# The expert map one unit earlier, with added constant products, in a fused attention and expert layer

## What is computed

```python
xn = _layernorm(x, axis=-1)
# attention: 16 heads of 16, windows of 128 at a stride of 64, rows cut back to 512
qkv = (xn @ w_qkv + b_qkv)
probs = jax.nn.softmax(scores, axis=-1)
o = o @ w_out + b_out
# experts
topk_scores, topk_idx = jax.lax.top_k(scores, TOP_K)      # 2 of 8
hidden = jax.nn.silu(h1) * h2
y = jnp.sum(total_probs[..., None] * expert_out, axis=-2)
x = x + attention(xn) + experts(xn)
```

## Time and profile before

| | |
|---|---|
| median of 3 runs (lowest to highest) | 743.64 us (742.49 to 745.95) |
| the profiled execution | 746.3 us, span 744.5 us |
| its mean granted TensorE clock | 0.976 |
| PE busy | 666.6 us of 744.5 |
| DVE busy | 565.8 us of 744.5 |

### The profile page before, as it was taken

One profiled execution on the slowest core, in us unless ns is written; L12 is line 12 of the kernel. 1 busy time (PEld: TensorE's weight loads), 2 busy tenths in 40 slices (PEclk: granted clock), 3 DMA queues, 4 the chain that ended last, 5 costly groups with the idle time before them and its releaser, 6 DMA issues.

```text
span 744.5 us, 17166 instructions
## 1 busy us (share of the span) xinstructions
PE 666.6 (90%) x5648; PEld 517.6 (70%) x5649; DVE 565.8 (76%) x881; ACT 512.1 (69%) x886; POOL 307.7 (41%) x334
## 2 busy tenths in 40 slices
PE   0686786969999999999999999999988998989995
PEld 0564564847878787778777887888766676767674
DVE  4758899657777777777777787778758879797984
ACT  4665486556767676767676767666756787978885
POOL 3000373422544454445444544454411244656654
PEclk9999798869999999999999999999999999999999
DMA  9894688370111111111111111111136777976740
GB/s 289 262 241 163 155 287 279 87 254 28 54 45 49 49 51 47 49 49 49 49 50 49 49 49 49 49 49 48 51 103 188 219 228 197 265 212 188 202 158 29
DMA packets 66351, 92.56 MB, mean 124 GB/s; under 512 B 6432, under 2 KB 53408, under 8 KB 66304
## 3 DMA queue, kind: packets, MB, share of 16 engines
q1 hardware_dynamic: 57872, 70.40, 31.7%
q0 software_dynamic: 6864, 18.75, 7.9%
q10 hardware_dynamic: 1568, 2.76, 1.2%
HBM read 59.06 MB, written 32.83 MB: 123 GB/s over the span
## 4 chain that ended last, share of the span: by engine, by line
PE 64%; DVE 11%; ACT 9%; issue 8%; DMA 3%; POOL 3%; SPq 1%; ACTq 0%; DVEq 0%; POOLq 0%
PE PS L1266 57%; PE PS L1516 4%; DVE SMALL L960 3%; ACT WORK L803 3%; PE PS L1494 2%; DVE XN L1122 1%; ACT QS L798 1%; DVE WALL L954 1%; DMA XN<-in_x 1%; POOL OTS L603 1%; DVE WORK L1032 1%; DVE WORK L1025 1%; DMA KS<-parts_scratch 1%; DVE WALL L978 1%; ACT WORK L731 1%
## 5 line engine op out<-in xcount | busy, mean ns | idle before, releaser
L370 DVE TENSOR_TENSOR WS<-WALL,WS 128x1024 fp32r<-128x1024 f32 x144 | 176.4, 1225 | 91.1 <-ACT WS L886 90.5
L1266 PE MATMUL PS<-WS,XTS 128*128 128x512 f32 x852 | 236.4, 413 | 2.4 <-DVE XTS L954 2.3
L1266 PEld LDWEIGHTS PS<-WS,XTS 128*128 128x128 f32 x852 | 151.6, 191 | 46.8 <-DVE XTS L954 14.9
L886 ACT ACTIVATE WS<-WALL 128x1024 fp32r x144 | 152.2, 1058 | 41.5 <-issue 39.3
L1266 PE MATMUL PS<-WALL,WORK 128*128 x568 | 136.2, 383 | 0.8 <-ACT WORK L902 0.8
L666 POOL DMA_INDIRECT WORK<-xn_scratch,WORK x72 | 101.2, 1406 | 31.6 <-issue 21.4
L1266 PEld LDWEIGHTS PS<-WALL,WORK 128*128 128x128 f32 x568 | 102.2, 190 | 12.9 <-issue 1.0
L603 POOL TENSOR_TENSOR OTS<-SIDE,XN 128x256 f32<-128x256 f32 x31 | 26.2, 845 | 195.7 <-DVE XN L1122 116.1
L670 POOL DMA_INDIRECT ys_scratch<-SIDE,WORK x36 | 42.0, 1165 | 118.6 <-ACT SIDE L912 118.6
L960 DVE TENSOR_REDUCE SMALL<-PS 128x8 f32<-128x1024 f32 x64 | 77.4, 1209 | 13.5 <-PE PS L1266 12.9
L803 ACT ACTIVATE WORK<-PS 128x512 f32<-128x512 f32 x128 | 69.4, 595 | 20.3 <-PE PS L1266 16.6
(11 more groups left out here) (142 smaller groups left out, 1008.6 us busy)
## 6 DMA issues: line engine op xcount, KB each, us to landing
WALL<-in_wexp SPq DMA_DIRECT2D x28, 384.0 KB, 7.0
WALL<-ys_scratch SPq DMA_DIRECT2D x16, 512.0 KB, 7.0
parts_scratch<-WORK SPq DMA_DIRECT2D x32, 240.0 KB, 2.4
QS<-parts_scratch SPq DMA_DIRECT2D x16, 480.0 KB, 4.5
XN<-in_x SPq DMA_DIRECT2D x4, 1024.0 KB, 12.3
xn_scratch<-XN SPq DMA_DIRECT2D x4, 1024.0 KB, 7.5
WALL<-in_x SPq DMA_DIRECT2D x8, 512.0 KB, 5.6
KS<-parts_scratch SPq DMA_DIRECT2D x16, 240.0 KB, 3.8
```

The source lines that it names most:

```text
L370: eng.tensor_tensor(out=WS[:, 1 - k, half, 1], in0=weights, in1=WS[:, 1 - k, half, 0].bitcast(F32), op=ALU.subtract).then_inc(low_ready[ha ...
L886: act.activation(WS[:, 1 - k, half, 0], weights, ACT.Copy).then_inc(high_ready[half], 1)
L1266: return pe.matmul(o, a, b, start=start, stop=stop)
```

## The change

The map's products are written behind unit 3 of batch 1 on PE, behind its projection; they were behind unit 4, ahead of unit 5. DVE takes and finishes the map in unit 4 (`take_map` was there already, `finish_map` was in unit 5). `keep_warm` is a new function of PE alone: products of the constants `IDF` and `WOUT` whose result nobody reads. Two of them stand ahead of every even unit from batch 0's unit 4 to batch 1's unit 6 (six places), behind a wait for `r_free`; two more stand at the entry of the expert phase and three on either side of the last projection, which now follows the first two `tokens` and has its reciprocal and division in halves. `rows_out` is one semaphore for each batch: ACT waits for the first before `high_part(1, 1, 0)`, DVE for the second before `low_part(1, 1, 0)`. ACT's `high_part(0, 0, 1)` moves behind the two `take_xt`.

```diff
-MAP_UNIT = 4
+MAP_UNIT = 3
+WARM_FROM = 4
...
         @block.scalar
...
                 high_part(0, 0, 0)
-                high_part(0, 0, 1)
                 act.wait_ge(probs_ready, c["ST"].now() + 2)
...
                 take_xt(0, 0)
                 take_xt(1, 1)
-                act.wait_ge(rows_out, 16 * EXTRA)
+                high_part(0, 0, 1)
+                act.wait_ge(rows_out[0], 16)
                 high_part(1, 1, 0)
...
         @block.vector
...
-                        if u == MAP_UNIT:
+                        if u == MAP_UNIT + 1:
                             take_map()
-                        if u == MAP_UNIT + 1:
                             finish_map()
...
-                    if last and u == UNITS - 1:
-                        invert_last()
+                    if ends(b) and u == UNITS - 1:
+                        invert_halves()
...
-                if ends(b):
-                    if not last:
-                        invert()
+                if last:
                     project(b, NWIN - 1)
...
                 low_part(dve, 0, 0, 0)
-                dve.wait_ge(r_free, c["R"].now() + 1)
...
                 low_xt(0, 0)
                 low_xt(1, 1)
+                project(EXTRA - 1, NWIN - 1)
+                dve.wait_ge(r_free, c["R"].now() + 1)
                 low_part(dve, 0, 0, 1)
+                dve.wait_ge(rows_out[1], 16)
                 low_part(dve, 1, 1, 0)
                 hidden(0, 0)
...
         @block.tensor
...
+            def keep_warm(o, n):
+
+                for _ in range(n):
+                    mm(o, IDF[:], WOUT[:, 0, :])
...
                 for u in range(UNITS):
+                    if first is not None and u % 2 == 0 and b * UNITS + u >= WARM_FROM:
+                        pe.wait_ge(r_free, c["R"].now() + 1)
+                        keep_warm(R_BANK[:, 0:D], 2)
...
-                    if first == 1 and u == MAP_UNIT:
-                        slot_map()
-                    if first == 1 and u == MAP_UNIT + 1:
+                    if first == 1 and u == MAP_UNIT + 2:
                         pe.wait_ge(map_taken, 1)
                     if u % 2 == 1 and (u > 1 or (b and b != EXTRA)):
                         project()
-                if ends:
+                    if first == 1 and u == MAP_UNIT:
+                        slot_map()
+                if last:
                     project()
...
-                pe.wait_ge(r_full, c["R"].now())
+                pe.wait_ge(w_free, c["W"].now() + 1)
+                keep_warm(W_BANK[:, 0:D], 2)
...
                 tokens(0, 0)
                 tokens(1, 1)
+                keep_warm(W_BANK[:, 0:D], 3)
+                project()
+                keep_warm(W_BANK[:, 0:D], 3)
                 up(0, 0, 0)
                 up(0, 0, 1)
```

More of the change, by code:

```diff
@@ L329, in layer @@
         xt_full, xt_high, xt_free = sem("xt_full"), sem("xt_high"), sem("xt_free")
-        rows_out = sem("rows_out")
+        rows_out = [sem(f"rows_out{b}") for b in range(EXTRA)]
         high_ready = [sem("high_ready0"), sem("high_ready1")]
@@ L483, in keep @@
                 t = slice(b * TB, (b + 1) * TB)
-                sp.dma_start(rv[:, t, :], XN[:, t, :]).then_inc(rows_out, 16)
+                sp.dma_start(rv[:, t, :], XN[:, t, :]).then_inc(rows_out[b], 16)
             begin(0)
@@ L496, in _ @@
             keep(1)
-            sp.wait_ge(rows_out, 16 * EXTRA)
+            for b in range(EXTRA):
+                sp.wait_ge(rows_out[b], 16)
             sp.wait_ge(y_stored, 1)
@@ L600, in divide @@
                 pool.wait_ge(sides_ready, 2 * w + 2)
-                pool.wait_ge(recip_ready, w + 1)
+                pool.wait_ge(recip_ready, w + 1 + (w >= EXTRA * NWIN))
                 wait_some(pool, r_full, w)
@@ L604, in divide, with divide_halves @@
                                    ).then_inc(turned_ready, 1)
+            def divide_halves(w):
+                pool.wait_ge(sides_ready, 2 * w + 2)
+                pool.wait_ge(r_full, w)
+                for k in range(NC_D):
+                    pool.wait_ge(recip_ready, w + 1 + (w >= EXTRA * NWIN) + k)
+                    pool.tensor_tensor(out=OTS[:, k, :], in0=SIDE[:, k * P:(k + 1) * P],
+                                       in1=DENS[:, k * P:(k + 1) * P], op=ALU.mult).then_inc(turned_ready, 1)
             def combine(t, first, ready):
@@ L678, in _ @@
             divide(6)
-            divide(7)
+            divide_halves(7)
             pool.wait_ge(xt_full, 1)
@@ L698, in _ @@
                         divide(b * NWIN + n)
[L699 to L704, removed]
+            divide_halves(B * NWIN - 1)
         @block.scalar
@@ L808, in sides @@
                 act.wait_ge(o_full, n)
-                wait_some(act, turned_ready, n - 1)
+                wait_some(act, turned_ready, n - 1 + (n > EXTRA * NWIN))
                 act.activation(SIDE[:], O_SUMS, ACT.Copy).then_inc(sides_ready, 1)
@@ L1122, in invert, with invert_halves @@
                 dve.reciprocal(out=DENS, in_=DENS).then_inc(recip_ready, 1)
-            def invert_last():
+            def invert_halves():
                 n = c["O"].add()
@@ L1400, in project @@
             def project():
-                pe.wait_ge(turned_ready, c["R"].now() + 1)
-                pe.wait_ge(r_free, c["R"].now() + 1)
+                n = c["R"].now()
+                before = n + (n >= EXTRA * NWIN)
+                pe.wait_ge(turned_ready, before + 1)
+                pe.wait_ge(r_free, n + 1)
                 for ch in range(NC_D):
-                    if c["R"].now() == B * NWIN - 1 and ch:
-                        pe.wait_ge(turned_ready, B * NWIN + ch)
+                    if n in (EXTRA * NWIN - 1, B * NWIN - 1) and ch:
+                        pe.wait_ge(turned_ready, before + 2)
                     last = mm(R_BANK[:, 0:D], OTS[:, ch, :], WOUT[:, ch, :], ch == 0, ch == NC_D - 1)
@@ L1436, in batch @@
             def batch(b, first=None):
-                par, last, ends = b % 2, b == LAST, b in (EXTRA - 1, LAST)
+                par, last = b % 2, b == LAST
                 for u in range(UNITS):
+                    if first is not None and u % 2 == 0 and b * UNITS + u >= WARM_FROM:
+                        pe.wait_ge(r_free, c["R"].now() + 1)
+                        keep_warm(R_BANK[:, 0:D], 2)
                     if not last:
```

## The result

The changed kernel takes 767.34 us (766.68 to 768.43, 4 runs), the kernel before in the same comparison 744.80 us (742.49 to 746.86, 4 runs): a ratio of 1.0301 with a 95% interval of 1.0276 to 1.0325, 22.5 us slower. The prediction was 764.8 us, 752 to 770, which is 21.2 us more than the 743.64 us that it started from. The profiled execution has a span of 766.0 us, 21.5 more than before.

A forecast was written before the change was run, and what follows sets the result against it. DVE was taken as the limit from 92 to 126 us, kept full by PE's lead. Even units 15.8, map 3.0 and entry 2.4 sum to 21.2 us, bringing the median of 743.64 to about 764.8 us, range 752 to 770.

The forecast's parts named there:

- What bounds the stage: From 92 to 126 us DVE is the limit, busy 32.81 of 34.00 us, and PE waits for it.
- The lead is lost by the wait: At even units PE can't begin before DVE ends the unit before, so DVE idles for PE's next products.
- The even units: DVE stalls at batch 0's units 4 and 6, batch 1's units 0 and 2: 15.8 us, between 10.6 and 17.1.
- The map: Behind unit 3 of batch 1: starts 1.4 us earlier, but unit 4's scores, maximum and reciprocal queue behind it; net 3.0 us lost.
- The entry: Start of the expert phase: the last projection follows the token tiles and the rows' store is waited for; 2.4 us lost.
- the cover: Batch 1's units 4 to 7 end within 13.16 us of the map's end, hiding unit 6's wait; otherwise it costs 2 us.
- the rows' store: At the entry, SP's store of the rows needs the 5.66 us that it needed before.
- The signs: Changed profile: DVE idle 2 to 5 us at even units, map directly behind POOL's places, loads at about 165.5 us.
- One sign of being wrong: First token tile not coming 13 us behind the last experts' loads but waiting for the attention work.
- The rival with the upper clock: Products keep PE's clock up through the batches; stalls 10.6, map 3.0, entry about 1: 14.6 us, 758 us; chance 0.22.
- The faster rival: PE's clock was the price; DVE doesn't wait in even units, and 7.7 us are gained: 736 us; chance 0.05.

The follow-up runs named there:

- a1: Changed kernel without the r_free waits and the two constant products at the six even units; new map place and entry stay: 750.82 us, ratio 1.0058.
- c4: As a1, but with the wait and its two products at batch 1's unit 2 alone: 756.36 us, ratio 1.0143.
- b2: As a1, but with the map behind unit 4's scores: 744.33 us, ratio 0.9993.
- c1: Changed kernel, all as it is, but with the map behind unit 4's scores: 763.56 us, ratio 1.0219.
- c3: As a1, with six constant products added between unit 3's projection and the map: 749.85 us, ratio 1.0053.
- a4: Changed kernel with the map back behind unit 4 and its lists finished in unit 5; waits, products and new entry stay: 767.92 us, ratio 1.0288.
- b1: Kernel before with the changed kernel's entry alone; map in its old place, nothing at the even units: 748.50 us, ratio 1.0040.
- b4: As b2, but without the eight constant products of the entry: 743.47 us, ratio 0.9984.
- c2: Kernel before with only the r_free waits and two products ahead of the six even units; map and entry as before: 767.54 us, ratio 1.0293.
- b3: Kernel before with only the map moved behind unit 4's scores and its lists finished in unit 4: 745.14 us, ratio 0.9998.

## Why the prediction was right, step by step

**What bounds the stage: shown.** DVE was the limit from 92 us to the map, and it had no slack: with the waits and products gone (a1) 18.1 us come back, with one wait and its pair (c4) 5 us go.

**The lead is lost by the wait and not by the products: shown.** Measured on a1, the waits alone cost 11.4 us, the products alone 3.3, both together 18.1. What PE makes for the next unit and what DVE does last in this one overlapped before; the wait makes them follow each other.

**The even units, 15.8 us: measured 15.7.** The terms were 5.6, 2.1, 3.6 and 4.5, and came out as 4.3, 2.0, 5.0 and 4.5. For unit 4 of batch 0 I had added 0.9 for ScalarE's chain, which had slack, and the clock rose before the scores. In batch 1's unit 0 I took the middle between full and half clock, and it was half; I also forgot ScalarE's part, 0.53 us with its wait, between the queries and keys and DVE's split. The errors cancel, which is luck. One slip besides: for unit 4 of batch 0, 92.81 and 2.1 + 1.7 + 1.0 make 97.6 and not 97.5, and 4.9 us and not 4.7.

**The map, 3.0 us: measured 5.2 (21.24 less 16.0).** The start of the map (1.4 us early in the sum, 1.6 measured against the shift of 16.0) and what is queued behind it (4.4 net in the sum, 4.3 measured) were right; a1, b2 and c1 show that the second is unit 4's scores, maximum and reciprocal. The term that is missing is the map's clock:

```profile
152.00:159.00 7.00, 6.61 (x65) 0.59 0.47 125
...
181.00:186.00 5.00, 4.47 (x23) 1.00 0.25 68
```

In the first stretch, the map's, the granted clock is 0.59, in the second, the entry's, 1.00. PE had waited for POOL's places for 3.26 us, the map started at the lower of its two levels (1.2 GHz), and 4.2 us became 6.7. In the kernel before, PE went into the map straight from unit 4 at 1.00. c3 shows that it is this gap: filled, the map takes 4.2 us. The other runs agree: 4.2 us where PE goes into the map from work at full clock (a4, b1, b4, c2), 5.5 to 6.7 behind waits of 2.2 to 3.6 us. By the Trainium skill (TensorE: Matmul & The Clock Gate, "HAM oscillation — how this bites in real kernels") waits between bursts of products bring the lower clock back; the trace agrees here and ahead of three of the four pairs of constant products. I had used that rule for the products and not for the map that I had moved behind a wait.

**The entry, 2.4 us: measured 0.2.** The token tiles came 0.6 us late of the loads (13.79 us in place of 13.16, because the attention work with unit 6's stall, 3.4 us, now ended last: the cover was gone by that much), and the first hidden tile 0.4 us earlier behind them. Two things make the difference. The mis-sized term is the rows' store: I took 5.66 us from issue to release, which in the kernel before lay beside the end of the experts' loads (DMA share 0.91 and 0.80 in the 4 us from 158), and in the changed kernel, with 0.43 and 0.74 from 184, DVE went on 3.77 us after the issue. In the twelve other kernels it was 3.62 to 3.89. (The 3.4 us in b1's expectation are counted from the end of the issue.) That the loads beside it made the difference was not tried by itself, but b3 and c2 speak for it: they have the entry of the kernel before, issue the store 16.2 and 13.8 us behind the loads in place of 12.7, and both show 3.62. The other thing is the clock. b1 shows that the entry does cost 2.0 us where PE has waited for the weights; in the changed kernel the late attention work kept PE busy, and the clock was 1.00. I had not foreseen that the entry is cheap where the attention work ends last.

**The signs.** DVE was idle 2.6 to 5.0 us in the four even units, the map stood behind POOL's places, and DVE waited 1.8 us for the rows' store, as foreseen. The loads came at 167.74 and not at 165.5. One sign of being wrong did appear: the token tiles waited for the attention work, 0.6 us beyond the 13.16. The sum had priced batch 1's unit 6 at nothing as long as the cover held, and it didn't hold.

So the mechanism was right for the even units, which are three quarters of the cost, and two smaller terms were wrong by 2.2 us each, in opposite directions. That the sum of 21.2 us came out so close to the 21.5 of the spans (22.4 by the ratio) is in that part luck. **The rival with the upper clock** (758 us) failed at its first step: two constant products for each even unit don't keep the clock up when the wait in front of them leaves PE idle for 4.5 to 9.2 us; 0.84 is the mean clock from 92 to 126 us, and it was 0.92 before. **The faster rival** needed DVE not to wait; from 84 to 180 us it waited 30.3 us for what PE had made (21.0 and 9.3 in the view of its waits). The entry's cost in b1 was 2.0 us in the trace and 3.0 by the ratio, whose interval (1.8 to 4.2) holds both.

## What to carry to other kernels

Before you put a wait into an engine's queue, ask what lead it gives up: with single buffers the producer's lead over the consumer is the only overlap that there is, and a wait on the consumer's last work of a step turns it into a sum of both, in each step. Work that is to hold the clock up must be ready before the idle stretch and not behind the wait that causes it. And when you move a step to where its inputs come last, price it at the lower clock and count what is queued behind it; here the map gained 1.6 us of start and lost 6.8.

## What was not expected of the hardware

TensorE's clock made the same 64 small products last from 4.2 to 6.7 us, and the sixth of a percent by which the best kernel is faster is smaller than that one difference. The store of one batch's rows took 5.66 us from issue to the engine that waited for it in the kernel before, beside the last experts' loads, and 3.62 to 3.89 us in the thirteen other kernels, in which it was issued 13.8 us or more behind them.
